# Linear attention beside a quantised projection on one core: scores in one piece, state next to inter, V in the queries' bank

## The reference

```python
q = softmax(be * heads(xn @ Wq.T + bq)); k = softmax(be * heads(xn @ Wk.T + bk))   # 64 heads of 8
v = heads(xn @ Wv.T + bv)
kv = cumsum(einsum('zsD,zsd->zsDd', k, v), axis=1); kn = cumsum(k, axis=1)
att = (einsum('zsD,zsDd->zsd', q, kv) / sum(q * kn)) @ Wo.T + bo
ffn = einsum('bsi,oi->bso', fp8(clip(xn / in_scale)) * in_scale, w_fp8 * w_scale) + bias
out = x + att + ffn
```

## Time and profile before

| | |
|---|---|
| median of 3 runs | 1173.98 us (1173.4 to 1174.12) |
| profiled execution, its span | 1173.3 us, 1171.5 us |
| TensorE, its weight loads | 1117.6 us (95%), 629.9 us |
| VectorE, ScalarE, GpSimd | 969.3 us, 898.9 us, 462.8 us |
| DMA | 104.39 MB, queue q1 42.3% of 16 engines |
| chain that ended last | PE 93%, DMA 2%, VectorE 2%, ScalarE 1%, issue 1% |

### The profile page before, as it was taken

How to read it: one execution, slowest core, us unless ns; L and a number is a source line. 1 busy time by engine, 2 the same in 40 slices (tenths; PEclk the granted TensorE clock), 3 DMA queues, 4 the chain that set the end, 5 groups by cost and what they waited for, 6 DMA issues and landing times.

```text
span 1171.5 us, 57412 instructions
## 1 busy us (share of the span) xinstructions
PE 1117.6 (95%) x24103; PEld 629.9 (54%) x24103; DVE 969.3 (83%) x1975; ACT 898.9 (77%) x1933; POOL 462.8 (40%) x714
## 2 busy tenths in 40 slices
PE   1589999999999999999999999999999999999996
PEld 1345555555555555555555555555555555555553
DVE  5688888888888888888888888888888888888883
ACT  1377887878878787887878788887878888787873
POOL 3234344344434434443443444344344434434420
PEclk9789999999999999999999999999999999999999
DMA  9223353345345544553554455345444333344331
GB/s 243 42 59 82 89 83 93 93 85 87 95 87 83 97 92 82 87 97 85 83 96 89 87 89 95 87 83 98 91 84 87 95 87 84 98 90 85 70 77 49
DMA packets 156469, 104.39 MB, mean 89 GB/s; under 512 B 111969, under 2 KB 128481, under 8 KB 156257
## 3 DMA queue, kind: packets, MB, share of 16 engines
q1 hardware_dynamic: 155536, 99.76, 42.3%
q10 hardware_dynamic: 720, 1.31, 0.3%
HBM read 40.20 MB, written 16.78 MB: 49 GB/s over the span
## 4 chain that ended last, share of the span: by engine, by line
PE 93%; DMA 2%; DVE 2%; ACT 1%; issue 1%; SPq 0%; POOL 0%; ACTq 0%; DVEq 0%
PE s_ps L948 11%; PE a_ps L1052 7%; PE k_ps L914 5%; PE vo_ps L914 5%; PE k_ps L1008 5%; PE k_ps L916 5%; PE k_ps L918 5%; PE k_ps L925 5%; PE k_ps L927 5%; PE k_ps L929 5%; PE q_ps L916 5%; PE vo_ps L918 5%; PE q_ps L918 5%; PE vo_ps L916 5%; PE q_ps L914 5%; PE a_ps L1037 4%
## 5 line engine op out<-in xcount | busy, mean ns | idle before, releaser
L488 ACT ACTIVATE st_pairs<-st_run 32x144 f32<-32x144 f32 x1008 | 331.0, 328 | 11.9
L424 POOL TENSOR_TENSOR w_own<-vp,cst 128x576 f32<-128x576 f32 x126 | 142.1, 1149 | 323.3 <-DVE vp L746 323.3
L548 ACT ACTIVATE q_heads<-qT,cst 128x512 f32<-128x512 f32 x256 | 163.9, 711 | 4.8 <-DVE qT L762 3.8
L690 DVE TENSOR_TENSOR att<-s_ps,cst 128x512 f32<-128x512 f32 x256 | 163.5, 680 | 0.0
L411 POOL TENSOR_TENSOR y_sum<-y,y_magic 128x512 f32<-128x512 f32 x64 | 81.5, 1274 | 153.4 <-DVE y_magic L648 153.4
L948 PE MATMUL s_ps<-q_heads,w_own 64*64 64x128 f32 x4096 | 141.3, 275 | 0.3 <-DVE att L690 0.3
L948 PEld LDWEIGHTS s_ps<-q_heads,w_own 64*64 64x64 f32 x4096 | 110.4, 132 | 54.0 <-issue 53.9
L530 ACT ACTIVATE w_own<-kT,cst 128x512 f32<-128x512 f32 x128 | 85.4, 714 | 62.3 <-DVE kT L730 62.3
L404 POOL TENSOR_TENSOR x_split<-xn,x_split 128x512 f16<-128x512 f32 x64 | 74.7, 1167 | 138.8 <-ACT x_split L471 138.8
L471 ACT ACTIVATE x_split<-xn 128x512 f16<-128x512 f32 x64 | 40.3, 630 | 94.3 <-DVE xn L637 94.3
L914 PE MATMUL k_ps<-w_hi,xT 128*128 128x512 f16 x256 | 98.6, 385 | 5.0 <-ACT k_ps L587 2.6
(11 more groups left out here) (152 smaller groups left out, 2277.2 us busy)
## 6 DMA issues: line engine op xcount, KB each, us to landing
v_groups<-vp SPq DMA_DIRECT2D x512, 36.0 KB, 3.2
x_in<-L_attn_x SPq DMA_DIRECT2D x64, 256.0 KB
x_res<-L_attn_x SPq DMA_DIRECT2D x64, 256.0 KB
out<-o_sb SPq DMA_DIRECT2D x64, 256.0 KB
w_own<-L_attn_Wk SPq DMA_DIRECT2D x1, 1024.0 KB, 12.6
w_own<-L_attn_Wq SPq DMA_DIRECT2D x1, 1024.0 KB, 14.6
w_own<-L_attn_Wv SPq DMA_DIRECT2D x1, 1024.0 KB, 16.4
att<-L_ffn_weight_fp SPq DMA_DIRECT2D x1, 1024.0 KB, 18.0
```

What stands on the lines that cost most here:

```text
L424: last = gp.tensor_tensor(v_pairs[:, c].rearrange("p h w -> p (h w)"), vp[:, t.parity].rearrange("p h w -> p (h w)"), pair_mask[:, c:c + 1 ...
L488: last = sc.activation(st_pairs[TOK * b:TOK * (b + 1), to, u::J, :, b % SP, :], st_run[TOK * u:TOK * (u + 1), b // SP, :, b % SP, :, :], A ...
L548: last = sc.activation(q_heads[:, i.parity, :, j, :], qT[:, i.parity, :, :], ACT.Copy, scale=head_mask[:, j:j + 1])
L690: v.tensor_tensor(att[:, c % 2, 4 * (c // 2):4 * (c // 2) + 4, :, :] .rearrange("p g j s -> p (g j) s"), s_ps[:, DM * (c % 2):DM * (c % 2 ...
```

## The change

Scores get four banks, s_ps of 4 x 512, and are computed in one piece. vo_ps and t_ps are gone: V goes into q_ps once Q's shift has read it, and the turned attention into the first bank of a_ps; the state's products go into the first two banks of s_ps once their masks are done. The state stands behind the queries, and inter directly behind it, ahead of quantised and output; values follow the output. K's pairs are made by GpSimd at the end of its body, from the same masks. On ScalarE y comes ahead of x_split, the seed of q_ps is written one body later (after V is scaled), ah and a quarter of the spreads (4) stand behind k_e, three quarters (12) behind q_e, ahead of K's seed and the query heads. On VectorE magic stands behind xn, the four masks with al between them ahead of Q's shift, then state and running state; the statistics are four steps ahead and near the body's end, with one more set in the set-up. The diff, without its unchanged parts, blank lines, renames of banks and the set-up (`top_ps`, `statistics(Step(0, 3))`):

```diff
@@ -218,16 +218,16 @@
...
-    vo_ps = ps("vo_ps", DM)
-    t_ps = ps("t_ps", DM)
-    s_ps = ps("s_ps", 2 * DM)
+    s_ps = ps("s_ps", SEQS * DM)
+    top_ps = s_ps[:, (SEQS - 1) * DM:SEQS * DM]
...
-    a_state = a_halves[:, :, 0:G // 2 * J * VW]
+    st_ps = s_ps[:, 0:SEQS // SP * DM].rearrange("p (n w) -> p n w", n=SEQS // SP)[:, :, 0:G // 2 * J * VW]
+    aT_ps = a_ps[:, 0:DM]
...
-                   ((q_ps, 0), (k_ps, 0), (vo_ps, 0), (s_ps, 0), (s_ps, 1), (a_ps, 0), (a_ps, 1))]
+                   ((q_ps, 0), (k_ps, 0), (s_ps, 2), (s_ps, 0), (s_ps, 1), (a_ps, 0), (a_ps, 1))]
...
@@ -426,15 +426,27 @@
...
+        def pair_keys(i):
+            pool.wait_ge(kT_ready, (i + 1).n)
+            if i.after(2):
+                pool.wait_ge(scores_done, (i - 1).n)
+            for c in range(SP):
+                last = gp.tensor_tensor(k_pairs[:, i.parity, :, c, :], kT[:, :, :],
+                                        pair_mask[:, c:c + 1, None].to_broadcast([P, G, TOK]), ALU.mult)
+            last.then_inc(kpairs_ready, 1)
...
+            if (i + 1).exists():
+                low_input(i + 1)
...
-            if (i + 1).exists():
-                low_input(i + 1)
...
+            if i.exists():
+                pair_keys(i)
...
@@ -467,12 +479,12 @@
...
-                act.wait_ge(x_turned, t.n * 16)
-            sc.activation(x_split[:, 0, :], xn[:, :], ACT.Copy).then_inc(xh_ready, 1)
-            if t.after(1):
...
+            if t.after(1):
+                act.wait_ge(x_turned, t.n * 16)
+            sc.activation(x_split[:, 0, :], xn[:, :], ACT.Copy).then_inc(xh_ready, 1)
...
@@ -495,6 +507,9 @@
...
+            if i.exists() and i.after(1):
+                act.wait_ge(vp_ready, i.n)
+                sc.activation(q_ps[:, :], bias[:, MQ, :], ACT.Copy).then_inc(qseed_ready, 1)
...
@@ -503,53 +518,46 @@
...
+                act.wait_ge(aT_done, (d + 1).n)
+                if d.after(1):
+                    act.wait_ge(o_done, d.n)
+                else:
+                    act.wait_ge(bvo_done, 1)
+                sc.activation(flat(ah[:, :, :]), aT_ps, ACT.Copy).then_inc(ah_ready, 1)
+            if fold:
+                act.wait_ge(bvT_done, 1)
+                sc.activation(flat(ah[:, :, :]), aT_ps, ACT.Copy).then_inc(bvh_ready, 1)
+            if last_weights:
+                last_weights()
+            if d.exists() and (i - 1).exists():
+                spread_state(d, range(3, 4))
+            if d.exists():
...
-            t = i - 2
-            if t.exists():
-                act.wait_ge(aT_done, (t + 1).n)
-                if t.after(1):
-                    act.wait_ge(o_done, t.n)
-                sc.activation(flat(ah[:, :, :]), t_ps[:, :], ACT.Copy).then_inc(ah_ready, 1)
-            if fold:
-                act.wait_ge(bvT_done, 1)
-                sc.activation(flat(ah[:, :, :]), t_ps[:, :], ACT.Copy).then_inc(bvh_ready, 1)
-            if last_weights:
-                last_weights()
-            if d.exists() and (i - 1).exists():
-                spread_state(d, range(SP, SEQS))
-            if i.exists():
-                act.wait_ge(kT_ready, (i + 1).n)
-                if i.after(2):
-                    act.wait_ge(scores_done, (i - 1).n * 2)
-                for c in range(SP):
-                    last = sc.activation(k_pairs[:, i.parity, :, c, :], kT[:, :, :], ACT.Copy,
-                                         scale=pair_mask[:, c:c + 1])
-                last.then_inc(kpairs_ready, 1)
+            if i.exists():
...
-                if (i + 1).exists():
-                    sc.activation(q_ps[:, :], bias[:, MQ, :], ACT.Copy).then_inc(qseed_ready, 1)
-                    if d.exists():
-                        act.wait_ge(o_ready, (d + 1).n)
-                    sc.activation(k_ps[:, :], bias[:, MK, :], ACT.Copy).then_inc(kseed_ready, 1)
+            if (i - 1).exists() and i.exists():
+                spread_state(i - 1, range(0, 3))
+            if (i + 1).exists():
+                if d.exists():
+                    act.wait_ge(o_ready, (d + 1).n)
+                sc.activation(k_ps[:, :], bias[:, MK, :], ACT.Copy).then_inc(kseed_ready, 1)
+            if i.exists():
...
-                    act.wait_ge(scores_done, (i - 1).n * 2)
+                    act.wait_ge(scores_done, (i - 1).n)
...
-            if (i - 1).exists() and i.exists():
-                spread_state(i - 1, range(SP))
...
@@ -765,47 +773,47 @@
...
-            if (i + 3).exists():
-                statistics(i + 3)
...
+            if (i + 1).exists():
+                magic(i + 1)
...
+            if d.exists():
+                split_low(d)
+            if t.exists():
+                mask_scores(t, 2)
+                mask_scores(t, 3)
+            if i.exists():
+                shift(i, q_ps, q_done, q_max, qmax_ready, q_shift, qshift_ready, qe_ready)
+            if fold:
+                dve.wait_ge(bvh_ready, 1)
+                v.tensor_tensor(flat(al[:, :, :]), aT_ps, flat(ah[:, :, :]), ALU.subtract)\
+                    .then_inc(bvl_ready, 1)
+            if last_weights:
+                last_weights()
...
-            if (i + 1).exists():
-                magic(i + 1)
-            if d.exists():
-                split_low(d)
-            if fold:
-                dve.wait_ge(bvh_ready, 1)
-                v.tensor_tensor(flat(al[:, :, :]), t_ps[:, :], flat(ah[:, :, :]), ALU.subtract)\
-                    .then_inc(bvl_ready, 1)
-            if last_weights:
-                last_weights()
+            if t.exists() and i.exists():
+                add_state(t)
...
-                shift(i, q_ps, q_done, q_max, qmax_ready, q_shift, qshift_ready, qe_ready)
-            if t.exists():
-                mask_scores(t, 2)
-                mask_scores(t, 3)
+                turn_queries(i)
...
-                v.scalar_tensor_tensor(bias[:, 3, :], vo_ps[:, :], out_dn[:, :], bias[:, 3, :],
+                v.scalar_tensor_tensor(bias[:, 3, :], q_ps[:, :], out_dn[:, :], bias[:, 3, :],
...
-            if i.exists():
-                turn_queries(i)
-            if t.exists() and i.exists():
-                add_state(t)
+            if (i + 4).exists():
+                statistics(i + 4)
...
@@ -930,22 +939,21 @@
...
-        def scores(t, half):
-            if half == 0:
-                pe.wait_ge(kpairs_ready, (t + 1).n)
-                pe.wait_ge(qheads_ready, (t + 1).n)
-                if t.after(1):
-                    pe.wait_ge(att_ready, t.n * 4)
-            else:
-                pe.wait_ge(att_ready, t.n * 4 + 2)
+        def scores(t):
+            pe.wait_ge(kpairs_ready, (t + 1).n)
+            pe.wait_ge(qheads_ready, (t + 1).n)
+            if t.after(1):
+                pe.wait_ge(att_ready, t.n * 4)
+                pe.wait_ge(masked_ready, t.n)
...
-            for q in range(4):
+            for q in range(2 * 4):
...
-                    g = GP * (4 * half + q) + gp
+                    g = GP * q + gp
...
-                        last = mm(s_ps[SP * TOK * gp:SP * TOK * (gp + 1), DM * n + P * q:DM * n + P * (q + 1)],
+                        col = DM * (SEQS // SP * (q // 4) + n) + P * (q % 4)
+                        last = mm(s_ps[SP * TOK * gp:SP * TOK * (gp + 1), col:col + P],
...
@@ -984,19 +991,14 @@
...
-            if i.after(1):
-                pe.wait_ge(vp_ready, i.n)
-            project(vo_ps, i, MV, seeded=False).then_inc(v_done, 1)
+            pe.wait_ge(qshift_ready, (i + 1).n)
+            project(q_ps, i, MV, seeded=False).then_inc(v_done, 1)
...
-            if t.after(1):
-                pe.wait_ge(al_ready, t.n)
-            else:
-                pe.wait_ge(bvl_ready, 1)
...
-                last = transpose(t_ps[:, :].rearrange("p (j b s) -> p b j s", b=SEQS, s=TOK)[:, b],
+                last = transpose(aT_ps.rearrange("p (j b s) -> p b j s", b=SEQS, s=TOK)[:, b],
...
@@ -1018,13 +1020,13 @@
...
-        def inter(t, more):
+        def inter(t):
...
-            if more:
-                pe.wait_ge(masked_ready, (t + 1).n)
+            if t.after(1):
+                pe.wait_ge(al_ready, t.n)
...
-                pe.wait_ge(an_ready, t.n)
+                pe.wait_ge(bvl_ready, 1)
...
@@ -1039,62 +1041,56 @@
...
-        def intra(t, h):
-            pe.wait_ge(att_ready, t.n * 4 + 2 * h + 2)
-            if h == 0:
-                for b in range(SEQS):
-                    pe.wait_ge(v_moved[t.parity][b], (t + 2).half * 16 * GP)
-                pe.sem_inc(pe_waited, 1)
-            for n in range(SEQS // SP):
-                for j in range(J):
-                    for u in range(J):
-                        last = mm(a_rows[TOK * u:TOK * (u + 1), n, h, :, j, :],
-                                  att[:, n, J * h + u, j, :],
-                                  v_groups[:, t.parity, :, n, J * h + u, j, :], start=False, stop=True,
-                                  skip_group_check=True)
-            if h == 1:
-                last.then_inc(a_done, 1)
```

(37 more changed lines are left out.)

30 lines of the change are left out of this document (15 added, 15 removed).

## The result

The changed kernel took 1184.87 us (median of 4, 1181.42 to 1190.32) against 1173.69 for the one before: ratio 1.0100, interval 1.0082 to 1.0117. The forecast was 1156, with a range of 1149 to 1175, so the sign was wrong. Its profiled execution has a span of 1180.4 against 1171.5. First the kernel before, then the one after, cut at the same places: third key product, 58 steps later, last key product, end. The columns are window and length, then busy time (instructions) of TensorE, its weight loads, VectorE, ScalarE and GpSimd, then granted clock, DMA share, GB/s.

The account below looks back on a forecast made before the run. TensorE's own stream was taken as the bound, 17.09 us a step. From 1173.3 us, minus 20.1 over 61 steps, plus 2.5 at the ends: 1155.7, at the median 1156; range 1149 to 1175.

Parts of the forecast that it names:

- TensorE's stream: TensorE's groups in one step: fewer entries and exits save 0.33 us, 17.09 to 16.76, 20.1 us over 61 steps.
- state to inter: TensorE boundary where inter now follows the state: 0.07 us a step saved, the middle between nothing and 0.14.
- the exit's 0.15: TensorE's gap between the state's last product and the transposes before the change: 0.15 us a step.
- Rival 1: State and inter adjoin on TensorE without a drain: 0.40 us a step, 24.4 us in all, 1152; chance 0.20.
- Does the rest keep up?: Hand layout of the other engines and loads against TensorE's 16.76 us step: all hidden, some with little to spare.
- The cover of 0.8 for V's pairs: GpSimd's V pairs end near 7 us into the step, wanted by TensorE at 7.8: thinnest cover, 0.8.
- rival 4: Thin covers (V pairs, ScalarE's ring) fail together, period stays at 16.9 us: 1164; chance 0.16.
- Rival 2: GpSimd's K pairs block VectorE's quantise in even steps, 1.6 us if behind both: 1170 to 1171; chance 0.10.
- rival 3's sign: VectorE's statistics waiting for x_in: under 20 us means no load trouble, over 60 with period above 17 means load-bound.
- Rival 3's ring: V's scaling, SyncE's load of x, statistics, quantise: 16.15 to 17.65 us; at 17.3 a step 1189; chance 0.14.
- The start, +2.1: First two steps: first about even, second +2.4 from inter and values waiting, less the step's 0.3: +2.1 us.
- The end, +0.4: Drain: last query heads 0.9 late behind 12 spreads, inter waits for al, second piece's waits go: +0.4 us.

Follow-up runs that it names:

- the last version: Changed kernel with residual's load, quantise and output earlier, 72 increments across steps 0 and 1, then 4 a step: 1163.20 us, ratio 0.9902.
- the run without either: Changed kernel with statistics three steps ahead again, placed between xn and magic on VectorE: 1191.67 us, ratio 1.0136.

## Why the prediction was wrong, step by step

- TensorE's stream, 0.33 a step less: right in itself. With the undisturbed length of every group the step went from 17.07 to 16.76, 0.31 less; the shortest steps of the changed kernel and 16.81 in the last version agree. Of its terms only state to inter (0.07) came out lower: the state with its exit took 0.81 before, and 0.78 now that inter follows, so 0.03 of the exit's 0.15 went. Rival 1 did not happen. The Trainium skill ("TensorEngine Tiling (Array Packing)", Key Properties) says that only a change of the tiling mode drains TensorE. By that the whole 0.14 would have gone, and 0.03 did; three semaphores stand between the two groups, and no run took them away.
- "Does the rest keep up?" was the step that failed. It asked whether each wait opens before TensorE comes to it, and put everything else at nothing. Against 16.76 a step the changed kernel loses 16.1 us in the 58 steps (intra 9.6, state 2.7, output 1.9, inter 1.3, queries 0.6) and 6.2 in the last three (inter 4.5, output 0.9, quantised 0.8). Three things lie behind it.
  - (a) TensorE's own supply of instructions was left out. At one place of the packets TensorE runs dry: most of the 6.2 in the last three steps, and part of the output's 1.9 in the others; and with the place kept there, 110 us between 17 and 128 increments. Before the change the four small groups stood apart, each behind large products, and now state and inter adjoin. That this is what makes the place a bad one is argued: the kernel before passed only half of the places, and no run held it at the others.
  - (b) The output was costed only as VectorE work. It comes later now, and the issue of its store and of the residual's load moved to the edge of the intra product with it: 1.40 in place of 1.26 in 61 steps, 9 us. I had read SyncE's issues only for the x ring. Both losses together are shown to be the cause: with the issues moved away and the place kept, the loop is 16.81.
  - (c) The cover of 0.8 for V's pairs, the thinnest in the layout, was too thin in some steps, a small part of rival 4: in the three steps where the state took 1.09 to 1.10, the pairs ended 7.8 to 7.9 into the step, against a median of 7.1 in undisturbed steps. They make 0.9 of the state's 2.7; ten steps of 0.86 to 0.95 make 1.2 more. This is read from the timeline.
- Rival 2 was right in its mechanism (1.03 for 0.43) and wrong in its path: nothing on TensorE waits for quantise. That the 0.6 on VectorE moves the store is argued; the last version took it away, but moved the output as well. Of the waits for x_in (rival 3's sign, 24.7) and for y the run without either says that they are not what costs time: its intra product took 1.43. Rival 3's ring did not bind.
- The start, +2.1: +1.4 measured. The second step is 2.2 longer (19.6 for 17.4), and the first 0.8 shorter, where the forecast had about even.
- The end, +0.4: +5.4 measured. In the runs whose end has a granted clock of 0.94 (0.95 before) it is 44.5 to 44.8, in those that have 0.90 it is 45.4 to 46.7. Counted from the last key product, in the kernel before and the run with 128 increments in front (44.8, 4.4 more): the last intra product comes 2.2 later, since quantised and output product stand between it and inter now; the last quantised product starts another 1.4 later, since its seed stands behind ah on ScalarE; and the last output product takes 3.7 in place of 2.8 at half the clock. The changed kernel itself (0.87) has 1.0 more, mostly from one more output product at half the clock, 4.1 in place of 2.7. This is read from the timelines; no run took these apart.
- Open: what in an issue of a 256 KB DMA holds TensorE up 0.8 to 0.9 us later. Taking it out of the intra product took the holes away (1.41 to 1.25); what it collides with was not shown.

## What to carry to other kernels

When an engine's unrolled stream is the bound, its instruction supply and the moments at which others issue DMAs belong to its path, even where no semaphore connects them. Count the instructions of a step: where the number creeps against the packets, as here 764 against about 768, a few steps may be long for no reason that the waits show, and a few increments beside large products move or fix the place. After a reorder look not only at whether each wait opens in time, but at what now starts beside the small products.

## What the hardware showed that I had not expected

- 111 semaphore increments at the start of a program decide between 1178 and 1284 us, through the place of the packets of 16384 B of instructions in the step.
- A semaphore increment costs TensorE 0.14 us where it has nothing else (128 in 18 us), and nothing seen between products of 0.22.
- The issue of a transposing DMA takes 5.38 in place of 1.26 right behind 512 KB on its queue, and a step 6 us more with it.
- The issue of a 256 KB DMA is followed 0.8 to 0.9 us later by a hole of 0.1 to 0.25 us where TensorE then runs its 128x36 products: 1.24 or 1.76 for the same 128 of them.
